# Six of eight trees fetch their leaf rows instead of four, with their sums on GpSimd, twelve row slots and a new order of calls

## What is computed

```python
logits = x @ W_in.T + b_in                      # 8 trees x 255 nodes
decisions = (logits > 0)
acts = silu(logits)
current = 0; dmap = one_hot(current)
for d in range(7):
    current = child of current by its decision  # left or right
    dmap = dmap + one_hot(current)
out = (acts * dmap).reshape(B, 8 * 255) @ W_out.T
h = h + out
```

## Time and profile before

| | us |
|---|---|
| median of 3 runs | 2026.34 (2025.54 to 2026.86) |
| the profiled execution, device time | 2028.2 |
| its span, first to last instruction | 2026.4 |
| mean granted clock of TensorE, share of full | 0.991 |

### The profile page before, as it was taken

How to read it: one execution, slowest core, us unless ns; L and a number is a source line. 1 busy time by engine, 2 the same in 40 slices (tenths; PEclk the granted TensorE clock), 3 DMA queues, 4 the chain that set the end, 5 groups by cost and what they waited for, 6 DMA issues and landing times. The chain is left out here.

```text
span 2026.4 us, 41146 instructions
## 1 busy us (share of the span) xinstructions
PE 1973.2 (97%) x12488; PEld 1858.1 (92%) x12488; DVE 1702.8 (84%) x4210; ACT 1397.2 (69%) x3085; POOL 1001.6 (49%) x1001
## 2 busy tenths in 40 slices
PE   6799999999999999999999999999999999999997
PEld 5689999999999999999999999999999999999986
DVE  5598888898888898888898888898888898888875
ACT  5467776677776676776676776676776776776764
POOL 2675445545445545445545545545545545545544
PEclk8999999999999999999999999999999999999999
DMA  4423223223222223223233223232223233222222
GB/s 131 108 75 93 76 77 82 79 72 90 77 75 81 78 76 87 74 77 80 75 83 84 75 76 82 73 86 83 75 75 81 74 87 83 75 75 79 61 68 80
DMA packets 81999, 163.12 MB, mean 80 GB/s; under 512 B 17102, under 2 KB 48048, under 8 KB 81968
## 3 DMA queue, kind: packets, MB, share of 16 engines
q0 software_dynamic: 40960, 103.02, 19.3%
q1 hardware_dynamic: 41008, 59.71, 10.3%
HBM read 148.76 MB, written 13.90 MB: 80 GB/s over the span
## 5 line engine op out<-in xcount | busy, mean ns | idle before, releaser
L483 POOL DMA_INDIRECT leaf_rows<-leaf_table,leaf_at x512 | 582.2, 1137 | 156.0 <-issue 156.0
L861 DVE TENSOR_TENSOR hid_lo<-hid,hid_hi 128x392 fp32r<-128x392 f32 (+1 forms) x256 | 255.3, 997 | 77.3 <-ACT hid_hi L551 77.2
L1168 PE MATMUL out_acc<-hid_hi,outw_lo 128*128 128x392 f32 x768 | 300.3, 391 | 0.2 <-DVE hid_lo L861 0.2
L456 POOL TENSOR_TENSOR inv_root<-to_root,minus_half 98x8 f32<-98x8 f32 x64 | 95.7, 1495 | 412.7 <-DVE to_root L911 266.1
L1168 PE MATMUL hid_ps<-ffn_x,in_lo 128*128 128x392 f32 x768 | 272.1, 354 | 1.8 <-ACT hid L706 0.7
L1170 PE MATMUL out_acc<-hid_hi,outw_hi 128*128 128x392 f32 x768 | 263.4, 343 | 0.0
L1169 PE MATMUL hid_ps<-ffn_x,in_hi 128*128 128x392 f32 x768 | 262.8, 342 | 0.0
L1169 PE MATMUL out_acc<-hid_lo,outw_hi 128*128 128x392 f32 x768 | 262.2, 341 | 0.0
L1170 PE MATMUL hid_ps<-ffn_x,in_hi 128*128 128x392 f32 x768 | 261.4, 340 | 0.0
L496 POOL TENSOR_TENSOR row_sum<-leaf_rows,row_sum 98x1024 f32<-98x1024 f32 x96 | 221.3, 2305 | 40.3 <-ACT leaf_rows L743 34.6
L482 POOL TENSOR_TENSOR held<-minus_half 98x1 f32<-98x1 f32 x128 | 35.7, 279 | 373.6 <-ACT v_full L637 199.6
(11 more groups left out here) (142 smaller groups left out, 5854.6 us busy)
## 6 DMA issues: line engine op xcount, KB each, us to landing
x_raw<-x SPq DMA_DIRECT2D x192, 196.0 KB, 2.4
out<-out_stage SPq DMA_DIRECT2D x32, 392.0 KB
leaf_rows<-leaf_table,leaf_at POOLq DMA_INDIRECT x512
leaf_table<-leaf_rows SPq DMA_DIRECT2D x4, 256.5 KB, 4.2
out_stage<-in_w SPq DMA_DIRECT2D x4, 256.0 KB
tok_major<-tok_w SPq DMA_DIRECT2D x3, 256.0 KB, 4.3
late_raw<-out_w SPq DMA_DIRECT2D x6, 128.0 KB
u<-uv_w SPq DMA_DIRECT2D x1, 576.0 KB, 4.2
```

What stands on the lines that cost most here:

```text
L483: pool.indirect_dma_start(row_slot(s, g), None, table, bass.IndirectOffsetOnAxis(ap=leaf_at[:, s, g:g + 1], axis=0), element_offset=s * P ...
L861: dve.tensor_tensor(out, src, hi.bitcast(F32), ALU.subtract).then_inc(done, 1)
L1168: pe.matmul(out, w[1], x_parts[0], start=start, stop=False)
```

## The change

`GATHERED` goes from 4 to 6, so trees 4 and 5 lose their leaf halves on PE, ACT and DVE and get eight more fetches, two more calls each of `find_leaf`, `leaf_number`, `leaf_dots`, `leaf_silu`, `scale_rows`, and two more `sum_rows` (five in all) in each unit. `ROW_SLOTS` goes from 8 to 12: three trees held. The number of weight pieces at the start falls from 14 to 12, and the waits of `fetch_rows` follow the slots. The lists of calls of POOL, ACT, DVE and PE are all in another order; on POOL the fetches of trees 1 (second half) to 5 now stand in the pass of the loop after that of tree 0, on PE the boundary of the pass lies after `find_leaf(i, 1)`.

```diff
-GATHERED = 4
+GATHERED = 6
-ROW_SLOTS = 8
+ROW_SLOTS = 12
-LATE_SPLITS = (((0, 1), (2,), (3,), (4,), (5,)), ((6,), (7,), (8, 9), (10, 11), (12, 13)))
+LATE_SPLITS = (((0, 1), (2,), (3,), (4,), (5,)), ((6,), (7,), (8, 9), (10, 11), ()))
...
                     elif not first(i):
-                        pool.wait_ge(rows_summed, SUMS * i + s + 1 - TREES_HELD)
+                        pool.wait_ge(rows_summed, SUMS * i + s + 1 + TREES_HELD - GATHERED)
```

POOL's list after the change, whole (the one before is in the code above):

```diff
             def body(p, i, n, nx):
+                fetch_rows(p, 1, 2)
+                fetch_rows(p, 1, 3)
+                fetch_rows(p, 2, 0)
+                fetch_rows(p, 2, 2)
+                fetch_rows(p, 2, 1)
+                fetch_rows(p, 3, 0)
+                fetch_rows(p, 2, 3)
+                fetch_rows(p, 3, 1)
+                fetch_rows(p, 3, 2)
+                sum_rows(p, 1)
+                fetch_rows(p, 3, 3)
+                fetch_rows(p, 4, 0)
+                fetch_rows(p, 4, 2)
+                fetch_rows(p, 4, 3)
+                fetch_rows(p, 4, 1)
+                sum_rows(p, 2)
+                fetch_rows(p, 5, 0)
+                fetch_rows(p, 5, 2)
+                fetch_rows(p, 5, 1)
+                fetch_rows(p, 5, 3)
+                norm_roots(i, 1)
+                sum_rows(p, 3)
+                sum_rows(p, 4)
+                norm_roots(n, 0)
                 late_splits(i, n, 0)
+                sum_rows(p, 5)
                 late_splits(i, n, 1)
                 fetch_rows(i, 0, 0)
+                fetch_rows(i, 0, 3)
                 late_splits(i, n, 2)
                 fetch_rows(i, 0, 1)
                 fetch_rows(i, 0, 2)
                 fetch_rows(i, 1, 0, n)
+                late_splits(i, n, 3)
+                late_splits(i, n, 4)
                 fetch_rows(i, 1, 1)
```

More of the change, by code:

```diff
@@ L756, in body @@
             def body(p, i, n, nx):
-                silu_tree(p, 7, 1)
+                hid_high(p, 6)
+                norm_apply(i, 1, 0)
+                norm_apply(i, 1, 1)
+                norm_apply(i, 1, 2)
+                norm_apply(i, 1, 3)
+                copy_h(n, 0)
+                copy_h(n, 1)
                 ffn_x_high(i, 0)
                 ffn_x_high(i, 1)
-                silu_tree(p, 7, 0)
-                copy_h(n, 0)
-                copy_h(n, 1)
-                scale_rows(p, 3)
+                scale_rows(p, 4)
+                leaf_silu(p, 5)
+                scale_rows(p, 5)
+                x_high(nx, 0)
                 hid_high(p, 7)
@@ L767, in body @@
                 silu_tree(i, 1, 0)
+                norm_apply(n, 0, 1)
                 leaf_number(i, 0)
-                norm_apply(n, 0, 1)
                 make_xn(n, 0)
@@ L1076, in body @@
             def body(p, i, n, nx):
+                mask(p, 7)
+                hid_low(p, 6)
+                ffn_x_low(i, 0)
+                ffn_x_low(i, 1)
                 norm_stats(n, 0, 0)
@@ L1419, in body @@
             def body(p, i, n, nx):
+                tree_logits(p, 4, 0)
+                tree_visits(p, 2)
+                tree_out(p, 0, 0)
+                turn_normed(i, 0)
+                tree_out(p, 0, 1)
+                turn_normed(i, 1)
+                make_base(i)
+                make_v(i, 0)
+                tree_visits(p, 3)
+                find_leaf(p, 2)
+                tree_out(p, 1, 0)
+                make_v(i, 1)
+                tree_visits(p, 4)
+                find_leaf(p, 3)
+                make_v(i, 2)
+                tree_out(p, 1, 1)
+                make_v(i, 3)
                 make_u(i, 0)
-                tree_visits(p, 4)
-                tree_logits(p, 5, 1)
+                tree_logits(p, 5, 0)
+                tree_out(p, 2, 0)
+                make_u(i, 1)
+                find_leaf(p, 4)
                 scores(i, 0)
-                make_u(i, 1)
+                tree_out(p, 2, 1)
                 tree_logits(p, 6, 0)
                 scores(i, 1)
+                make_u(i, 2)
+                make_u(i, 3)
+                tree_logits(p, 6, 1)
+                tree_out(p, 3, 0)
                 tree_visits(p, 5)
-                make_u(i, 2)
-                tree_logits(p, 6, 1)
-                make_u(i, 3)
-                tree_out(p, 3, 0)
                 mix(i, 0)
                 mix(i, 1)
+                tree_out(p, 3, 1)
+                tree_visits(p, 6)
+                find_leaf(p, 5)
                 mix(i, 2)
                 mix(i, 3)
-                tree_visits(p, 6)
-                tree_out(p, 3, 1)
+                embed(n, 0)
                 tree_logits(p, 7, 0)
```

181 lines of the change are left out of this document (68 added, 113 removed).

## The result

The changed kernel takes **2174.5 us** (median of 4 runs, 2164.4 to 2186.1) against 2026.4 before: a ratio of 1.073, 95% interval 1.069 to 1.077. The forecast was 1987.5, its range ended at 2050. The profiled execution took 2176.6, its span is 2174.7, 148.3 more than before.

What follows compares the result with a forecast made beforehand. PE was taken to bound the loop: 57.0 + 1.1 + 1.3 = 59.4 us a unit. 28 x (60.98 - 59.4) = 44, + 5 + 1.6 - 12 = 39 us less gave 1987.5 us, range 1930 to 2050.

Steps and rivals of the forecast that it cites:

- standstill: DVE stopped while POOL sums rows: 1.0 us a sum, five sums a unit, bringing DVE from 51.6 to 56.7 us.
- PE's floor: The shortest possible unit, set by PE's work alone with no waits: 57.0 us.
- Rival (b): Sums and DVE collide: 1.6 us of standstill a sum, 61.9 us a unit, 2060 us in all; chance 0.18.
- point of decision: Where the rival of colliding sums decides: from 60.7 us a unit, which is 1.4 us of standstill a sum.
- Second chain: POOL's fetches up to tree 5, then dot product and normalisations: PE waits 1.3 us at turn_ffn_x, bounds 0 to 3.5.
- The fetches just fit: Up to turn_ffn_x: 38.0 us of chain against 38.8 of PE work at clean price; 2.5 us late at mean price.
- First chain: First norm, turn of h to last ACT step: 10.8 us against 9.7 on PE; wait 1.1 at turn_xn, bounds 0 to 2.3.
- PE's own work: PE's work in a unit falls from 60.93 to 57.0 us: 24 matmuls at 0.178 us go, two find_leaf come.
- Start: Before the loop's unit 3: fewer pieces split on POOL, two more trees of rows; 5 us less, bounds 12 less, 5 more.
- Tail: After unit 31: eight more fetches, a further sum, small writes; 12 us more, bounds 4 and 14; 1.6 gained beside PE work.

Runs made afterwards that it cites:

- with fills: The changed kernel with each row sum replaced by a tiny write and two GpSimd fills of nearly the same length: 2075.5 us.
- The kernel with the fills and without the fetches: The changed kernel with row sums replaced by a tiny write and two GpSimd fills, and the eight fetches of trees 4 and 5 left out: 2019.1 us.
- the kernel with the added wait and no fetches: The changed kernel with tree 3's sum waiting for tree 5's last dot product, and the eight fetches of trees 4 and 5 left out: 2106.5 us.
- narrow dots: The changed kernel with its 24 dot products a unit over 8 of 257 columns: 2202.3 us.
- the sum behind the roots: The changed kernel with sums 2, 3 and 4 moved later or earlier, sum 4 behind norm_roots, and find_leaf(i, 0) behind tree 3's logits: 2329.0 us.
- four attempts at the order: The changed kernel with sum 3 after the last dot: 2111.2 us; plus update_h first: 2119.9; or plus sum 2 earlier: 2100.5; that plus two more moves: 2329.0.

## Why the prediction was wrong

**The step that failed is the one that puts the standstill into a load.** "With five sums at 1.0 it is 56.7. That is 0.3 under PE's floor": the number is right (DVE 56.3 us, without collisions 51.9 against 51.6 forecast, so 0.88 us a sum) and the conclusion wrong. A standstill of 2 us doesn't spread over a unit. It hits one instruction, and what counts is who waits for that one. From the load the forecast took no wait of PE at all; measured are 5.6 us of waits a unit in place of its 2.4, with 2.50 behind the last dot, 1.15 behind the first dot of tree 3 and 0.89 behind the moments. DVE has 8.5 us of idle time in a unit of 64.85, about as much as before, and is on the path at three places all the same. The kernel before shows the reverse: 2.7 us of standstill at no cost. The trace of before had both rows that were needed, the last dot through at 1053.40 and the sum beginning at 1053.49; the new list of DVE puts one more `x_low`, 0.48 us, ahead of the last dots, and this meeting could have been read off it.

**Rival (b)** named the right engines, direction and mechanism, but was priced as a load too: 1.6 us a sum, 61.9 us a unit, 2060 us. Measured are 0.88 a sum and 65.16 a unit. Its point of decision (1.4 us a sum) was never reached, and the kernel is slower nevertheless.

**Second chain, 1.3 us at `turn_ffn_x`.** As a term it was good: with the standstill gone it is 1.86 us with fills in the unit shown, inside its bounds, and taking the fetches away saves 1.7 us a unit. In the changed kernel it is hidden behind the collision, which makes the wait 2.50: leaving out the fetches there saves 0.5 us a unit. "The fetches just fit" was right of fetches (1115 ns), and left out what a sum between the last fetch and its dot does.

**First chain, 1.1 us at `turn_xn`.** No such wait, but not because the chain is short. For the unit from 1203.07 it takes 12.1 us, not 10.8 (turn of h at 1198.61, last step of ACT to 1210.73). PE comes later still, at 1210.90, since three short waits hold it up on the way: 0.89 at `visits`, 0.36 at the logits, 0.71 at `find_leaf`. A fourth, 0.60, follows at another `find_leaf`. They are for DVE and ACT inside the trees, 2.6 us in all. The forecast looked at two long chains and took the short ones for covered. The kernel with the fills and without the fetches still has the last three of them, with 0.25 at `visits` and 0.32 at `turn_ffn_x`, and so takes 60.46 us a unit and not 57.0.

**PE's own work, 57.0.** As the price of the work it stands (0.178 us a matmul; 374 to 376 instructions; the sums above close with it). What was missing is that each wait costs about 0.25 us over its length, and that shorter work meets new waits: leaving the same matmuls out of the old kernel gave 2.05 us a unit and not 4.27, for three new waits. The new list keeps less: without standstill and without the added fetches it has 0.5 us (60.98 - 60.46) of the 3.9 that PE saves.

**Start, 5 less** (bounds 12 less, 5 more): 14.9 more. With fills it is 3.2 more, inside the bounds; the rest is standstill of DVE, which was not priced for the start at all. **Tail, 10.4 more net**: 16.3 more. With fills 9.8 more. So both come out inside their bounds or near them but for the same term.

**Not in the sum at all: the clock.** Over PE's work, its waits and 0.25 us for each, the 28 units have at most 32 us left here, some 22 in the kernel with the added wait and no fetches, 109 with narrow dots and 160 with the sum behind the roots. This is an estimate, from the waits and lengths of the units of each trace.

The 148 us so are: 99 of standstill (after to fills), 56 of fetches that then show, and a rest of -7, by which the kernel with fills and no fetches is faster than the one before. The split depends on the order of removal: the fetches alone are worth 21, the standstill behind them 134. Open is whether another order of the calls would bring the 60.5 down to the 58.9 of the old list; four attempts at the order found one that is 74 us better than the change and none that beats the kernel before.

## What to carry to other kernels

Price interference by the instruction that it hits and by who waits for that instruction, not by its sum over a unit; ask of each pair of engines whether the same event releases both, because then they meet in every unit or in none, and a call of half a microsecond can decide which. When the bound engine gets less to do, list all that it meets sooner, the short waits too, and test the gain by leaving the work out before writing what replaces it. A wait added ahead of a long, unhurried instruction can be worth far more than it costs.
